# Dilated attention: scores computed once, exponentials with accumulated row sums, transposed on TensorE

## What is computed

```python
H, D, DIL, SEG = 16, 256, (1, 2, 4), (128, 128, 128)
def _mha(x, Wqkv, bqkv, Wo, bo):
    q, k, v = jnp.split(x @ Wqkv.T + bqkv, 3, axis=-1)
    scores = jnp.einsum('...qhd,...khd->...hqk', q, k) * scale
    a = jax.nn.softmax(scores, axis=-1)
    o = jnp.einsum('...hqk,...khd->...qhd', a, v).reshape(*lead, S, D)
    return o @ Wo.T + bo
...
pairs = [(br, off) for br in range(n) for off in range(DIL[br])][:n]
for br, off in pairs:
    ...
    xs = x[:, off::r, :].reshape(b_, -1, S, D_)
    att = _mha(xs, Wqkv[br], bqkv[br], Wout[br], bout[br])
```

## Time and profile before

| | |
|---|---|
| median of three runs | 4507.68 us (4504.64 to 4517.12) |
| the profiled execution's own time | 4505.73 us |
| its span | 4503.9 us |
| the attention stage in it, first scores to last output sum | 1266.8 to 2423.4 us |
| TensorE matmul / weight load busy over the whole span | 91% / 79% |
| VectorE / ScalarE / GpSimd busy | 77% / 52% / 28% |
| mean granted TensorE clock | 0.969 |

### The profile page before, as it was taken

How to read it: one execution, slowest core, us unless ns; L and a number is a source line. 1 busy time by engine, 2 the same in 40 slices (tenths; PEclk the granted TensorE clock), 3 DMA queues, 4 the chain that set the end, 5 groups by cost and what they waited for, 6 DMA issues and landing times. The chain is left out here.

```text
span 4503.9 us, 92992 instructions
## 1 busy us (share of the span) xinstructions
PE 4082.2 (91%) x36328; PEld 3536.5 (79%) x36328; DVE 3461.4 (77%) x7394; ACT 2331.1 (52%) x3029; POOL 1252.9 (28%) x850
## 2 busy tenths in 40 slices
PE   6999999999779898999985999999999979787879
PEld 5888888888667777777774888888888867686756
DVE  7998999999656666666665999999999858445667
ACT  4777766766544444444441776766677733221123
POOL 3444444444200000000001444444444401011200
PEclk9999999999999999999997999999999989898989
DMA  1000000000000000000001000000000012359332
GB/s 58 15 15 15 15 16 15 15 15 17 26 24 16 17 21 12 21 12 21 16 7 63 10 15 16 15 15 19 17 16 15 10 60 89 133 196 250 103 95 77
DMA packets 175379, 180.63 MB, mean 40 GB/s; under 512 B 9680, under 2 KB 167632, under 8 KB 174928
## 3 DMA queue, kind: packets, MB, share of 16 engines
q1 hardware_dynamic: 174928, 174.37, 12.4%
HBM read 98.84 MB, written 75.50 MB: 39 GB/s over the span
## 5 line engine op out<-in xcount | busy, mean ns | idle before, releaser
L358 POOL TENSOR_TENSOR f_grid<-f_sim 128x1024 f32<-128x1024 f32 x512 | 1023.3, 2028 | 1201.3 <-DVE f_q L657 1193.2
L647 DVE SCALAR_TENSOR_TENSOR f_q<-f_grid,f_te,f_p_dot 128x1024 f32<-128x1024 f32 x512 | 620.8, 1274 | 148.0 <-ACT f_grid L516 119.3
L657 DVE SCALAR_TENSOR_TENSOR f_q<-f_q,f_rz,f_grid 128x1024 f32<-128x1024 f32 x512 | 622.9, 1280 | 0.0
L516 ACT ACTIVATE f_grid<-f_grid,f_negm 128x1024 f32<-128x1024 f32 x512 | 538.5, 1134 | 0.0
L435 PE MATMUL f_p_wT<-f_ident,f_q 128*128 128x128 f32 x4096 | 478.8, 273 | 3.8 <-ACT f_q L535 3.7
L1285 DVE TENSOR_REDUCE a_mneg<-a_p_s 128x4 f32<-128x512 f32 x512 | 318.0, 684 | 203.0 <-PE a_p_s L1104 203.0
L435 PEld LDWEIGHTS f_p_wT<-f_ident,f_q 128*128 128x128 f32 x4096 | 455.7, 140 | 20.3 <-ACT f_q L535 4.1
L535 ACT ACTIVATE f_q<-f_q 128x4096 f32<-128x4096 f32 x128 | 464.0, 3625 | 4.7 <-DVE f_q L657 4.5
L446 PE MATMUL f_p_y<-f_wdn,f_hs 128*128 128x256 f32 x2048 | 462.9, 379 | 1.4 <-ACT f_hs L530 1.4
L451 PE MATMUL f_p_y<-f_eup,f_wT 128*128 128x256 f32 x2048 | 462.8, 379 | 0.0
L446 PEld LDWEIGHTS f_p_y<-f_wdn,f_hs 128*128 128x128 f32 x2048 | 383.5, 190 | 54.0 <-ACT f_hs L530 1.8
(11 more groups left out here) (369 smaller groups left out, 9306.5 us busy)
## 6 DMA issues: line engine op xcount, KB each, us to landing
x_f<-f_yt SPq DMA_DIRECT2D x64, 256.0 KB, 2.2
f_xt<-x SPq DMA_DIRECT2D x32, 256.0 KB, 2.8
a_xt<-x_f SPq DMA_DIRECT2D x16, 512.0 KB, 3.9
x_a<-a_yt SPq DMA_DIRECT2D x16, 512.0 KB, 3.5
f_xt<-x_a SPq DMA_DIRECT2D x32, 256.0 KB, 2.8
c_xt<-x_f SPq DMA_DIRECT2D x16, 512.0 KB, 4.7
x_c<-c_yt SPq DMA_DIRECT2D x16, 512.0 KB, 3.2
b1p_xt<-x_c SPq DMA_DIRECT2D x16, 512.0 KB, 4.3
```

The source lines that it names most:

```text
L358: last = pool.tensor_tensor(grid[v][:, hd, :].rearrange("p (i j) -> p i j", i=XROWS), sx[:, hd, :].unsqueeze(2).to_broadcast([P, XROWS, KE ...
L516: last = act.activation(grid[v][:, hd, :], grid[v][:, hd, :], ACT.Exp, bias=negm[:, v, hd:hd + 1])
L647: d_mask.mark(dve.scalar_tensor_tensor(out=q[v][:, hd, :], in0=grid[v][:, hd, :], scalar=te[:, v, hd, TOP - 1:TOP], in1=p_dot[:], op0=ALU. ...
L657: last = dve.scalar_tensor_tensor(out=q[v][:, hd, :], in0=q[v][:, hd, :], scalar=rz[:, v, hd:hd + 1], in1=grid[v][:, hd, :], op0=ALU.mult, ...
```

## The change

Scores are computed once, query by key, and stay in their banks. Per bank, ScalarE runs four instructions of 128 x 128 (one a head) with the negated maximum of that head as its bias and the row sum as accumulated output `z`. The exponentials then have queries on partitions, so TensorE turns them, four 128 x 128 transposes a bank, through one PSUM bank `p_t`, and VectorE copies each turned bank to `exT`. The 128 x 16 row sums are inverted by VectorE (`inverse`), turned on TensorE (`turn_rz`), copied (`turned_rz`) and spread over 16 rows per head by a product with a constant (`repeat`), which ScalarE copies to SBUF as `rep`; `divide` is then one multiplication, and it is done one unit later. `attend` loses its half with the ones. `ex` and `z` have two buffers. The input is turned by quarters in units 0 to 3 and both its parts are made by VectorE; `put_out` moves to units 4 to 7. The projections of branch 1 are read in the strided order and written contiguously.

The diff, cut to its core. TensorE's program:

```diff
+                def turn_ex(t, i):
+                    a_ex.wait(pe, t, str(i))
+                    if i:
+                        d_ex.wait(pe, t, str(i - 1))
+                    elif (t - 1).exists():
+                        d_rzT.wait(pe, t - 1)
+                    for n in range(QUAD):
+                        last = pe.transpose(p_t[:, n, :], ex[t.step % 2][:, i, n, :], ident[:])
+                    t_ex.mark(last, str(i))
+                def turn_rz(t):
+                    d_rz.wait(pe, t)
+                    d_ex.wait(pe, t, "3")
+                    t_rz.mark(pe.transpose(p_t[0:SLOT, 0, :], rz[:], ident[:]))
...
+                def repeat(t):
+                    d_rzT.wait(pe, t)
...
+                    for c in range(DC):
+                        last = pe.matmul(p_rep[:, c, :], spread[0:SLOT, c, :], rzT[0:SLOT, :], start=True, stop=True)
+                    t_rep.mark(last)
...
                 def step(t):
                     scores(t)
-                    if (t - 1).exists():
-                        attend(t - 1)
-                    if ahead:
-                        project(t + SEGS)
-                    maxima(t)
-                    scores_t(t)
+                    if (t - 2).exists():
+                        a_rep.wait(pe, t - 2)
                     if ahead:
                         value(t + SEGS)
+                    if before:
+                        turn_ex(t - 1, 1)
+                    if ahead:
+                        project(t + SEGS, 0)
+                    if before:
+                        turn_ex(t - 1, 2)
+                    if ahead:
+                        project(t + SEGS, 1)
+                    if before:
+                        turn_ex(t - 1, 3)
                     x_free(t)
-                    if u < 2 and (r + 1).exists(last=rows):
+                    if u < SEGS and (r + 1).exists(last=rows):
                         turn_h(r + 1, u)
-                    if OUT_AT <= u < OUT_AT + 4 and (r - 1).exists():
-                        put_out(r - 1, u - OUT_AT)
+                    if u >= SEGS and (r - 1).exists():
+                        put_out(r - 1, u - SEGS)
+                    if before:
+                        turn_rz(t - 1)
+                        attend(t - 1)
+                        repeat(t - 1)
+                    turn_ex(t, 0)
```

ScalarE's:

```diff
                 def exps(t):
-                    if (t - 1).exists():
-                        t_av.wait(act, t - 1)
+                    if (t - 2).exists():
+                        t_ex.wait(act, t - 2, "3")
                     for i in range(QUAD):
-                        t_st.wait(act, t, str(i))
-                        a_ex.mark(act.activation(ex[:, i, :, :], p_s[i][:], ACT.Exp), str(i))
+                        d_max.wait(act, t, str(i))
+                        for n in range(QUAD):
+                            last = act.activation(ex[t.step % 2][:, i, n, :], p_s[i][:, n, :], ACT.Exp,
+                                                  bias=mneg[:, i, n:n + 1], accum_out=z[t.step % 2][:, i, n:n + 1])
+                        a_ex.mark(last, str(i))
+                def repeat(t):
+                    t_rep.wait(act, t)
+                    if (t - 1).exists():
+                        d_o.wait(act, t - 1)
+                    a_rep.mark(act.copy(rep[:], p_rep))
...
                 def step(t):
...
-                    if ahead:
+                    exps(t)
+                    if (t - 1).exists():
+                        repeat(t - 1)
+                    if (t + SEGS).exists(last=units):
                         project(t + SEGS)
-                    exps(t)
-                    if ahead:
                         value(t + SEGS)
```

VectorE's:

```diff
                 def step(t):
-                    maxima(t)
-                    turned(t)
-                    if 1 <= u < 3 and (r + 1).exists(last=rows):
-                        turn_h(r + 1, u - 1)
-                    if (t - 1).exists():
-                        divide(t - 1)
+                    if (t - 2).exists():
+                        divide(t - 2)
+                    if before:
+                        inverse(t - 1)
+                        turned(t - 1, 0)
+                    maximum(t, 0)
+                    maximum(t, 1)
+                    if before:
+                        turned(t - 1, 1)
+                    maximum(t, 2)
+                    if before:
+                        turned(t - 1, 2)
+                    maximum(t, 3)
+                    if before:
+                        turned(t - 1, 3)
+                        turned_rz(t - 1)
+                        t_av.wait(dve, t - 1)
+                    if u < SEGS and (r + 1).exists(last=rows):
+                        turn_h(r + 1, u)
+                    if u >= SEGS and (r - 1).exists():
+                        put_out(r - 1, u - SEGS)
                     if (r + 2).exists(last=rows):
                         if u == 5:
                             statistics(r + 2)
                         if u == 7:
                             scale(r + 2)
```

More of the change, by code:

```diff
@@ L967, in dilated_attention @@
         SETUP = 4
+        quads = [str(b) for b in range(QUAD)]
         s_ld = [m.track(f"s_ld{k}", inc=16) for k in range(2)]
@@ L1184, in _ @@
                 for j in range(SEGS):
-                    project(first_unit + j)
+                    for c in range(DC):
+                        project(first_unit + j, c)
                     value(first_unit + j)
```

259 lines of the change are left out of this document (121 added, 138 removed).

## The result

The changed kernel takes 4632.51 us, median of 4 runs (4631.28 to 4632.91), against 4511.43 for the kernel before on the same chip: a ratio of 1.0274, 95% interval 1.0258 to 1.029, so 121 us slower. The forecast was 4538 us, 32 above before. The sign is right, but three quarters of the loss were not foreseen: the time lies in the wide range of 4445 to 4690 and outside the 4515 to 4600 that the forecast gave itself.

What follows compares the result with a forecast made beforehand. TensorE, nearly full, and the scores-maxima-exponentials loop bound it; the change replaces both with three nearly equal paths. Rows of 71.9 us against 70.07 give +29, setup and end +3, on 4505.7: 4538 us, range 4445 to 4690.

Steps and rivals of the forecast that it cites:

- ScalarE's pairs: ScalarE's exponentials: an ACTIVATE with its accumulator read takes 0.37 us, 16 of them 5.9 us a unit.
- the read that doesn't overlap: Rival on ScalarE: accumulator reads don't overlap, a pair takes 0.51 us, ScalarE closes every unit's loop, 4738 us; chance 0.15.
- The statistics' delay behind unit 5: VectorE's output sum and statistics in unit 5 delay the next unit's maxima, so its exponentials start 1.4 us later.
- The chain behind copy 3: Units 0 to 3: copy 3 ends at T + 3.91, next T at 8.25; T is the start of a unit's exponentials.
- VectorE after T: ... copy 1 1.12: VectorE's order after the exponentials start (T): maximum 1 until 0.50, copy 1 until 1.12, through copy 3 at 3.91 us.
- hidden up to E + 2.3: Branch 1's evacuations on ScalarE stand behind the exponentials and cost nothing until 2.3 us after their end E.
- Copies every 1.39: VectorE's copies of turned banks in each unit: copy 1 ends at 1.12, copy 2 at 2.52, copy 3 at 3.91 us.
- Turned sums to `attend` to spreading: TensorE's chain in units 0 to 3: turned sums until 4.15, `attend` 5.1, spreading 5.65 us after exponentials start.
- The scaling, 1.37, costs 0.9 likewise: VectorE's scaling of the input, behind unit 7, takes 1.37 us and delays the next exponentials by 0.9.
- stay hidden: GpSimd's and SP's waits for LayerNorm, loads and stores cost nothing, having a row of time.
- TensorE's own sum 8.55: TensorE's own work in a unit with an output product sums to 8.55 us.
- The second rival's 8.1: Rival: TensorE's order closes without holes, units 4 to 7 go at 8.1 us, 4450 us in all; chance 0.28.

Runs made afterwards that it cites:

- experiment 4: Changed kernel without accumulated row sums, the sums a constant 1 so the softmax is not normalised: 4630.79 us, ratio 1.0276.
- experiment 1: Changed kernel with TensorE's transposes of bank 1 moved ahead of the value product: 4585.48 us, ratio 1.0174.
- experiment 16: Changed kernel with the strided writes of before for branch 1's queries and keys: 4665.97 us, ratio 1.0346.
- experiment 3: Changed kernel with a needless VectorE memset of 0.17 us ahead of copies 2 and 3 in each unit: 4632.11 us, ratio 1.028.
- experiment 7: Kernel of experiment 6 with the spreading product issued one unit later and the value product behind the projections: 4536.74 us, ratio 1.0064.
- 9: Changed kernel with reciprocals spread by VectorE copies and turned by two transposes, orders as they are: 4589.83 us, ratio 1.0179.
- 2: Changed kernel with GpSimd's residual sum moved from unit 7 to unit 1 of the next row: 4625.45 us, ratio 1.0267.
- 6: Changed kernel with the edits of experiments 1 and 2, plus VectorE's statistics and scaling ahead of the turned sums' copy: 4559.47 us, ratio 1.0116.
- experiment 10: Kernel of experiment 8 with a loop body of 32 units instead of 16, one back edge instead of five: 4489.61 us, ratio 0.9957.
- 8: Kernel of experiment 7 with reciprocals spread by two VectorE copies and turned by two transposes, without turned sums: 4532.57 us, ratio 1.0053.
- experiment 15: Kernel of experiment 14 with the body written out over 64 units, no loop left in the stage: 4472.51 us, ratio 0.9918.
- 14: Kernel before with contiguous writes in branch 1 and a loop body of 32 units: 4477.31 us, ratio 0.9929.
- experiment 12: Kernel before with branch 1's queries and keys written contiguously from a strided PSUM read, nothing else: 4498.08 us, ratio 0.9968.

## Why the prediction was right in sign and wrong in size

**Right.**
- ScalarE's pairs. The first pair's interval is 1826.46 - 1826.11 = 0.35, 16 of them take 5.5 us; forecast 0.37 and 5.9. The read takes 0.09 of each interval (0.34, against 0.25 without it in experiment 4), the value that was chosen. Its rival, the read that doesn't overlap, is refuted, and experiment 4 shows that even the 5.5 us don't bound. The Trainium skill, ScalarE: Activation LUTs, section What ACT_TABLE_LOAD costs, gave an estimated 0.39 a pair and 6.2 us: the measurement is below both. (The read's 0.09 in that estimate is the prediction's, not the page's.)
- The statistics' delay behind unit 5: 10.91 - 9.36 = 1.55, forecast 1.4.
- Unit 6 goes at 9.36 and unit 4 at 9.53, forecast 9.15, in part by luck: the forecast had a chain of waits over 8.55 us of TensorE's work, and that work is 9.2 by itself (below).
- TensorE stays at the 2.4 GHz level (granted clock 0.98), and is busy for 87% of the stretch, below the 92% that the prediction named.
- The chain behind copy 3, within 0.2 us: 4.50 from its end to the next T, forecast 4.34.

**Wrong, step by step.**
- *"VectorE after T: ... copy 1 1.12"*, that is from 0.50 to 1.12: copy 1 starts at T + 1.10. This is the step that failed. The prediction put transposes 1 ahead of T without asking what stands before them in TensorE's program: the value product, and its wait for a bank that ScalarE empties last of all. The term for that wait is nothing in its sum. It is the largest part: 47 us by experiment 1. The same error stands in *"hidden up to E + 2.3"* for the evacuations. By it the slower, strided evacuation would have cost 0.6 us in two units a row, 19 us; experiment 16 shows 0.75 in two units and 0.6 in a third, 33 us, so nothing of it is hidden.
- *Copies every 1.39:* they take 1.51, since one bank `p_t` is emptied, refilled and read in turn. The prediction had this round (its transposes 2 start at 1.20, behind copy 1), and experiment 3 confirms that it, and not VectorE's work, sets the pace. It was sized too small: 0.62 for a copy, which is what one takes that follows another instruction without a gap, and 0.08 until TensorE starts, where 0.69 and 0.12 were measured. 0.25 us a unit.
- *Turned sums to `attend` to spreading* was priced nearly right (0.64 for the product's 0.55, 1.01 for `attend`'s 0.95), but the detour over TensorE was taken as unavoidable; ScalarE waits 154 us in all for it, and experiments 7 and 9 regain 23 and 43 us.
- *"The scaling, 1.37, costs 0.9 likewise":* it takes 2.61 beside GpSimd. Unit 7 is 11.22, forecast 10.05. That GpSimd's waits *"stay hidden"* was true of its waits, not of what it does to VectorE. 7 us.
- Keys: the scores of the unit behind unit 3 or 7 wait up to 0.6 us for the key evacuation (13.5 us in all, the L1106 row). Experiment 16, with slower keys, has 20.0. The prediction named no such wait.
- *TensorE's own sum 8.55* for units 4 to 7 and *"-0.25 us a unit"*: experiment 7 shows 9.2, against 8.79 before, so TensorE's work grows by 0.4 us. The largest miss is the projections, 1.27 in the sum and 1.68 there. The prediction read the term from weight loads, and a weight load can start ahead of its matmul. The matmuls of that same unit before show 1804.38 - 1802.89 = 1.49 for the projections and 0.2 for turning the maxima, where it had 1.27 and 0.42 (a term that it let go):

```profile
1802.89 0.50 PE L103 MATMUL a_p_pr<-a_hT0l,a_wq0h 128*128 128x512 f32 x1
...
1804.38 0.27 PE L1113 MATMUL a_p_mv<-a_ident,a_mpad 128*128 128x128 f32 x1
```

  Splitting the projections in two halves adds another 0.2, the four groups of transposes take 2.0 instead of 1.84 (0.38 to 0.58 each), the spreading 0.09 more. The second rival's 8.1 lies well below the result.
- *+3 for prologue and end:* from the last scores to the last output sum it takes 33.3 instead of 27.3.

The terms are those of one chain, and they don't add. Experiments 1, 2 and 6 together regain 73 us of the error of 94, experiment 1 by itself 47; experiment 7 regains 23 more, but by an order that the forecast did not assume either, so that the sum of 96 proves nothing.

**The change as such.** With these waits shortened and one back edge it stands at 4489.61 (experiment 10). The kernel before, given the contiguous writes and the longer body, is at 4477.31. By the starts of the matmuls, computing the scores once removes 2.6 us of TensorE work a unit and puts back about 3.1 in experiment 7 (transposes 2.0, sums and spreading 0.84, split projections 0.2). Experiment 10 turns and spreads in 0.14 what took 0.84, but its TensorE still waits for VectorE's copies ahead of the transposes (us in all, times, longest):

```profile
PE a_p_t L1120 <- DVE a_exT L1307: 74.0, 135, 1.7
```

In its units 4 to 7, 9.09 us long, the last matmul of the first projection half starts at 2138.06 and the transposes behind it at 2139.00, where 0.24 would do: 0.7 lost. Without that they would take an estimated 8.4, less than the 8.79 of before. So what is lost there is slack: one bank's turning needs ScalarE, TensorE and VectorE in turn. A second bank for `p_t` would be the next thing to try; it wasn't tried, and whether the change would then be a gain is open.

## What to carry to other kernels

When a step is forecast to start "when its data is there", read the program of its engine upwards: what stands before it, what that waits for, and which bank or buffer it needs back. Where several chains are of nearly one length, as in this kernel, an overlooked wait counts almost in full and a saving only in part. Read the prices of TensorE's groups from the starts of its matmuls, not from those of its weight loads. And split a large change: the part that looked like housekeeping, contiguous writes, was a gain by itself, and the rest the loss.

## What the runs showed of the hardware

- A loop's back edge costs this stage 3.5 us in the kernel before, some 4.3 in the changed one, 6.5 in experiment 7, 6.9 in 9 and 7.5 in 8, in the two units around it, on TensorE. Longer straight code has a small price: 69.3 us a row in experiment 15 and outside the loop of 14, 69.0 inside it. Still, 64 units without a loop are the fastest. Why the edge costs more in one kernel than in another stays open.
- VectorE's scaling of 128 x 256 from SBUF takes 0.41 us in the kernel before. Beside GpSimd's sum it takes 0.81, in 39 of the 56 of the changed kernel's row above; the others take 0.41, which makes the mean of 0.69; moving the sum brings it back to 0.41. VectorE's next multiplication, whose one input lies in PSUM, takes its usual 0.41 beside the same sum.
- ScalarE writes 128 x 512 to SBUF in 0.78 us contiguously and in some 1.25 where the writes alternate between two halves, 256 elements apart (queries of branch 1, with bias and scale); for keys it is 0.69 and 1.17. The mean of 1015 ns in experiment 12 is that of both branches. Reading PSUM with a stride of two instead costs nothing that shows: 0.78 and 0.69 for both branches in the changed kernel.
- An accumulator read is listed with 0.19 to 0.29 us but delays the next instruction by 0.09. The means by group, 401 and 242 ns, therefore add up to 0.64 for a pair that takes 0.34. The busy time of a stretch has no such double count: ScalarE's 143 of 200 us fall to 117 without the reads.
